# One core, attention and a mixture of experts: a longer ring of loaded tiles, one more border between batches, and last steps taken in another order

## What is computed

```python
x = layernorm(x + attention(x, W_Q, W_K, W_V))
logits = (x @ gate_w + gate_b) / 0.9
keep = the two experts with the highest logits
h = gelu(einsum('bsd,edf->bsef', x, w1) + b1)
y = einsum('bsef,efd->bsed', h, w2) + b2
f = sum over the kept experts of gate_prob * y
f = (f - mean) / sqrt(var + 1e-5) * ln_g + ln_b
out = layernorm(x + f)
```

## Time and profile before

| what | us |
|---|---|
| median of three runs (lowest, highest) | 259.19 (258.05, 260.06) |
| the profiled execution, its time | 257.17 |
| its span, first to last instruction | 255.4 |
| PE busy | 229.6 (90%) |
| DVE busy | 173.4 (68%) |
| ACT busy | 179.3 (70%) |
| POOL busy | 144.3 (57%) |

### The profile page before, as it was taken

How to read it: one execution, slowest core, us unless ns; L and a number is a source line. 1 busy time by engine, 2 the same in 40 slices (tenths; PEclk the granted TensorE clock), 3 DMA queues, 4 the chain that set the end, 5 groups by cost and what they waited for, 6 DMA issues and landing times.

```text
span 255.4 us, 7300 instructions
## 1 busy us (share of the span) xinstructions
PE 229.6 (90%) x1874; PEld 209.0 (82%) x1875; DVE 173.4 (68%) x958; ACT 179.3 (70%) x527; POOL 144.3 (57%) x165
## 2 busy tenths in 40 slices
PE   6988998999999799999999999999999999999100
PEld 3466876788787689999999999999999999999100
DVE  0146576787888888558953333366488999989884
ACT  3365857778675889977886555555555996599953
POOL 8400007357777777777877777775544545546500
PEclk9999999999999999999999999999999999999855
DMA  5999303023131545523328797868789686913275
GB/s 143 250 332 332 105 3 93 31 74 97 53 95 53 137 134 120 144 68 107 95 75 254 204 355 241 221 183 246 228 267 356 186 232 180 320 47 114 92 220 151
DMA packets 45105, 42.38 MB, mean 166 GB/s; under 512 B 5488, under 2 KB 34080, under 8 KB 45072
## 3 DMA queue, kind: packets, MB, share of 16 engines
q1 hardware_dynamic: 40224, 32.84, 45.2%
q0 software_dynamic: 4320, 8.92, 10.0%
q10 hardware_dynamic: 528, 0.26, 0.3%
HBM read 27.89 MB, written 12.01 MB: 156 GB/s over the span
## 4 chain that ended last, share of the span: by engine, by line
PE 78%; DVE 10%; ACT 5%; DVEq 2%; issue 2%; DMA 1%; ACTq 0%; SPq 0%
PE bank L595 26%; PE bank L584 25%; PE bank L435 6%; PE bank L462 4%; PE bank L502 3%; PE bank L421 3%; PE bank L483 2%; ACT rows L668 2%; PE bank L450 2%; ACT probs L676 2%; PE bank L426 2%; PE bank L592 2%; PE bank L416 1%; DMA wk<-in_L_attn_W_K_dram 1%; DVE sum_stats L1139 1%
## 5 line engine op out<-in xcount | busy, mean ns | idle before, releaser
L749 ACT ACTIVATE h<-bank,b_cols 128x128 f32<-128x128 f32 x284 | 81.6, 385 | 37.4 <-PE bank L584 37.0
L1340 POOL DMA_INDIRECT returned<-x,slot_back x71 | 71.3, 1004 | 43.0 <-DVE x L1120 33.2
L1335 POOL DMA_INDIRECT slots<-rows,slot_of x64 | 65.0, 1016 | 53.0 <-DVE rows L984 34.4
L595 PE MATMUL bank<-w_all,h 128*128 x568 | 78.5, 282 | 0.0
L584 PE MATMUL bank<-slot_xT,w_now 128*128 128x128 f32 x568 | 75.2, 275 | 0.1
L595 PEld LDWEIGHTS bank<-w_all,h 128*128 128x128 f32 x568 | 69.0, 192 | 0.8
L584 PEld LDWEIGHTS bank<-slot_xT,w_now 128*128 128x128 f32 x568 | 69.1, 192 | 0.3 <-DVE slot_xT L883 0.3
L881 DVE CAST slot_back<-slot_x 128x1 uint32<-128x1 f32 x71 | 10.4, 147 | 37.9 <-PE bank L584 37.8
L838 DVE TENSOR_REDUCE negmax<-bank 128x1 f32<-128x128 f32 (+3 forms) x32 | 14.7, 484 | 16.0 <-PE bank L436 15.8
L462 PEld LDWEIGHTS bank<-v,probsT 128*128 128x128 f32 x160 | 19.7, 192 | 5.7 <-issue 3.8
L1120 DVE TENSOR_SCALAR x<-bank,slot_gate 128x128 f32<-128x128 f32 x71 | 24.0, 341 | 0.2 <-PE bank L595 0.2
(11 more groups left out here) (155 smaller groups left out, 305.4 us busy)
## 6 DMA issues: line engine op xcount, KB each, us to landing
w_now<-in_L_ffn_w_dram SPq DMA_DIRECT2D x47, 256.0 KB, 3.6
slot_x<-slots SPq DMA_DIRECT2D x71, 65.0 KB
w_all<-in_L_ffn_w_dram SPq DMA_DIRECT2D x16, 256.0 KB, 5.9
pair<-returned SPq DMA_DIRECT2D x14, 256.0 KB, 3.2
rows<-rows SPq DMA_DIRECT2D x8, 256.0 KB, 3.0
x<-n_L_attn_embeddings_dram SPq DMA_DIRECT2D x7, 256.0 KB, 3.9
returned<-x,slot_back POOLq DMA_INDIRECT x71, 3.4
slots<-rows,slot_of POOLq DMA_INDIRECT x64, 2.3
```

The source lines that it names most:

```text
L595: m = nc.tensor.matmul(o, h[:, s % RING, c * P:(c + 1) * P], w2_c, start=False, stop=(c == FC - 1))
L749: m = nc.scalar.activation(h[:, s % RING, cols], bank_[:, cols], ACT.Gelu, bias=b1_cols[:, c:][:, bass.ds(first, 1)])
L1335: g_.indirect_dma_start(slots, bass.IndirectOffsetOnAxis(ap=slot_of[:, b, c:c + 1], axis=0), rows[:, k, b * TB + t, :], None).then_inc(dis ...
L1340: g_.indirect_dma_start(returned, bass.IndirectOffsetOnAxis(ap=slot_back[:, j:j + 1], axis=0), y[:, j % Y_RING, :], None).then_inc(y_retur ...
```

## The change

- The ring of loaded tiles has 24 places, not 8. The two small copies of `copy_slots` go: `weigh` and `give_back` read the gate and the row number from the loaded tile itself. For that the row numbers are written as integers. SP waits for the tile copy where it waited for the two small ones, and from tile 24 on also for the return of the tile 24 before.
- PE's loop over tiles 24 to 63 becomes straight-line code.
- A border after batch 4 is added (`WHOLE`: 39, 47, 55, 63, 67, 71), and the pairs of batches 4 and 5 are loaded ahead of tiles 62 and 70 (before: 70 and, for batch 5, behind the last tile's load).
- DVE's units begin a step later, take seven units of cost a step, stand in another order, and now hold batch 6's head; it goes out of `last_steps`.
- ACT's second root comes at tile 64, not 65.
- PE contracts tile 67 ahead of the expansion of tile 70, not behind it.

```diff
-    PARTS = (4 * 2, 6 * 2, 7 * 2, 7 * 2 + 1, 8 * 2)
+    PARTS = (4 * 2, 5 * 2, 6 * 2, 7 * 2, 7 * 2 + 1, 8 * 2)
...
-        slot_x = sb("slot_x", [P, UNROLL, ROW])
-        slot_back = sb("slot_back", [P, J], U32)
-        slot_gate = sb("slot_gate", [P, 2 * UNROLL])
+        SLOT_RING = 3 * UNROLL
+        slot_x = sb("slot_x", [P, SLOT_RING, ROW])
...
-        LOAD_AT = {b: WHOLE[0] + 15 + b for b in range(4)} | {b: WHOLE[1] + 10 + b for b in (4, 5)}
+        LOAD_AT = {b: WHOLE[0] + 15 + b for b in range(4)} | {b: WHOLE[b - 3] + 14 for b in (4, 5)}
...
-        FINAL_AT, FINAL_SHARE = WHOLE[0] + 7, 6
-        NORM_FROM, NORM_AT, OUT_AT, ROOT_AT = 2 * TB, 55, 67, (52, 65)
+        FINAL_AT, FINAL_SHARE = WHOLE[0] + 8, 7
+        NORM_FROM, NORM_AT, OUT_AT, ROOT_AT = 2 * TB, 55, 67, (52, 64)
...
-                    sp.wait_ge(slot_read, j - (UNROLL - 1))
+                    sp.wait_ge(slotT_ready, j - (UNROLL - 1))
                     sp.sem_inc(wait_held, 1)
+                    if j >= SLOT_RING:
+                        sp.wait_ge(y_returned[(j - SLOT_RING) % Y_RING], 16 * ((j - SLOT_RING) // Y_RING + 1))
...
-                    load_slots(s, at[s])
+                    load_slots(j % SLOT_RING, at[s])
...
-                            if b in (0, FIRST):
-                                wait_whole(0 if b < FIRST else 1)
+                            if b == 0 or b >= FIRST:
+                                wait_whole(max(b - 3, 0))
...
+                    if last and s == LAST - 1:
+                        contract(J - LAG, (J - LAG) % UNROLL, e[s + 1]).then_inc(step_done, 1)
...
-            with pe.Fori(BOUND, BODIES - 1) as i:
+            for i in range(BOUND, BODIES - 1):
                 body(i, late=True)
             body(BODIES - 1, late=True, last=True)
             e = expert_numbers(J, LAG)
-            for s in range(LAG):
+            for s in range(1, LAG):
                 contract(J - LAG + s, (J - LAG + s) % UNROLL, e[s]).then_inc(step_done, 1)
...
-                vec.tensor_copy(slot_back[:, bass.ds(j, 1)], slot_x[:, s % UNROLL, BACK:ROW])
-                vec.tensor_copy(slot_gate[:, j % (2 * UNROLL):j % (2 * UNROLL) + 1], slot_x[:, s % UNROLL, GATE:BACK]).then_inc(slot_read, 1)
                 vec.tensor_copy(slot_xT[:, s % RING, :], psT_of(j, s)).then_inc(slotT_ready, 1)
...
-                vec.tensor_scalar(y[:, j % Y_RING, :], psY(s), slot_gate[:, j % (2 * UNROLL):j % (2 * UNROLL) + 1], None, ALU.mult).then_inc(y_ready, 1)
+                vec.tensor_scalar(y[:, j % Y_RING, :], psY(s), slot_x[:, j % SLOT_RING, GATE:BACK], None, ALU.mult).then_inc(y_ready, 1)
...
-            FINAL += [(what, b, cost) for b in (2, 3) for what, cost in PLAIN]
-            FINAL += [(what, b, cost) for b in (4, 5) for what, cost in HEAD]
-            FINAL += [("centre", 4, 5), ("centre", 5, 5), ("root", 1, 3)]
+            FINAL += [(what, 2, cost) for what, cost in PLAIN]
+            FINAL += [(what, 4, cost) for what, cost in HEAD]
+            FINAL += [(what, 3, cost) for what, cost in PLAIN]
+            FINAL += [("centre", 4, 5)] + [(what, 5, cost) for what, cost in HEAD] + [("centre", 5, 5), ("root", 1, 3)]
             FINAL += [(what, b, cost) for b in (4, 5) for what, cost in FUSED[1:]]
+            FINAL += [(what, 6, cost) for what, cost in HEAD]
...
             def last_steps():
                 for q in range(finished_by(J), len(FINAL)):
                     final_unit(q)
-                add_pair(6)
-                take_moments(6)
                 finish_root(2)
...
-                g_.indirect_dma_start(returned, bass.IndirectOffsetOnAxis(ap=slot_back[:, j:j + 1], axis=0),
+                g_.indirect_dma_start(returned, bass.IndirectOffsetOnAxis(ap=slot_x[:, j % SLOT_RING, BACK:ROW].bitcast(U32), axis=0),
```

More of the change, by code:

```diff
@@ L219, in moe_block @@
         slot_loaded = [sem(f"slot_loaded{s}") for s in range(UNROLL)]
-        slot_read = sem("slot_read")
         wait_held = sem("wait_held")
@@ L304, in load_slots @@
             def load_slots(s, at):
-                sp.dma_start(slot_x[:, s, :], slots[bass.ds(at, P), :]).then_inc(slot_loaded[s], 16)
+                sp.dma_start(slot_x[:, s, :], slots[bass.ds(at, P), :]).then_inc(slot_loaded[s % UNROLL], 16)
             def load_pair(b):
@@ L392, in _ @@
                 load_w1(J - W1_LAG + k, e)
-            wait_whole(2)
+            wait_whole(3)
             load_pair(B - 2)
-            wait_whole(3)
+            wait_whole(4)
             load_pair(B - 1)
-            wait_whole(4)
+            wait_whole(5)
             load_pair(B)
@@ L501, in transpose_slots @@
                     pe.wait_ge(y_ready, i * UNROLL + (s - AHEAD - LAG - 3))
-                return nc.tensor.transpose(psT_of(i if not isinstance(i, int) else i * UNROLL + s, s), slot_x[:, s, 0:D], ident[:])
+                return nc.tensor.transpose(psT_of(i * UNROLL + s, s), slot_x[:, (i * UNROLL + s) % SLOT_RING, 0:D], ident[:])
             def step(b):
@@ L607, in body @@
                 tiles = LAST if last else UNROLL
-                e = expert_numbers(i * UNROLL, tiles)
+                e = expert_numbers(i * UNROLL, tiles + (1 if last else 0))
                 for s in range(FIRST_EXPANDED if first else 0, tiles):
@@ L744, in gelu @@
             def gelu(j, s, first):
-                act.wait_ge(step_done, j + 1)
+                act.wait_ge(step_done, j + 1 + (1 if isinstance(j, int) and j == J - 1 else 0))
                 bank_ = psH_first[s] if isinstance(j, int) and j < UNROLL else psH[s % 4]
@@ L1114, in weigh @@
             def weigh(i, s):
-                dve.wait_ge(step_done, i * UNROLL + (s + LAG + 1))
                 j = i * UNROLL + s
+                dve.wait_ge(step_done, j + LAG + (0 if j == J - LAG else 1))
                 if j >= Y_RING:
                     dve.wait_ge(y_returned[j % Y_RING], 16 * (j // Y_RING))
-                vec.tensor_scalar(y[:, j % Y_RING, :], psY(s), slot_gate[:, j % (2 * UNROLL):j % (2 * UNROLL) + 1], None, ALU.mult).then_inc(y_ready, 1)
+                vec.tensor_scalar(y[:, j % Y_RING, :], psY(s), slot_x[:, j % SLOT_RING, GATE:BACK], None, ALU.mult).then_inc(y_ready, 1)
             one = "p (t a) -> p t a"
@@ L1206, in final_unit @@
                     m = aggregate(b)
-                    if (b, again) in ((3, False), (5, False), (5, True)):
+                    if (b, again) in ((3, False), (5, False), (5, True), (6, False)):
                         m.then_inc(aggregated, 1)
@@ L1313, in _ @@
             for b in range(B):
-                g_.iota(rows[:, :, b * TB:(b + 1) * TB, BACK], [[N, TOPK], [1, TB]], base=b * S, channel_multiplier=TB,
+                g_.iota(rows[:].bitcast(I32)[:, :, b * TB:(b + 1) * TB, BACK], [[N, TOPK], [1, TB]], base=b * S, channel_multiplier=TB,
                         allow_small_or_imprecise_dtypes=True).then_inc(const_ready, 1)
@@ L1320, in _ @@
             pool.wait_ge(made, 4)
-            g_.iota(empty[:, :, BACK], [[P, BLOCKS]], base=TOPK * N, channel_multiplier=1,
+            g_.iota(empty[:].bitcast(I32)[:, :, BACK], [[P, BLOCKS]], base=TOPK * N, channel_multiplier=1,
                     allow_small_or_imprecise_dtypes=True).then_inc(const_ready, 1)
```

## The result

The changed kernel takes 260.36 us in the median of 20 runs (259.27 to 262.31), the kernel before beside it 258.68 us (257.04 to 260.39). The ratio is 1.0078, interval 1.0055 to 1.0101: it became 1.4 to 2.6 us slower, within the 1% named in the prediction, but clearly not a gain.

A forecast was written before the change was run, and what follows sets the result against it. TensorE's 2.005 us a tile bounds it to the last contraction, then VectorE's tail. Adding 0.2 for ScalarE's root, 0.1 for the table and 0.1 for pair 8 to the 259.19 us median gives 259.6, range 257.6 to 261.8.

The forecast's parts named there:

- rival C: TensorE at tiles 24 and 25: both loads 0.4 us late, both stall, + 0.5; time 260.0 to 260.7 us; chance 0.11.
- Ring, straight line, pace: Tile loop: ring saves VectorE 0.13 us a step, TensorE nothing; straight line costs nothing, pace stays 2.005 us a tile.
- Rival E: TensorE's tile loop: its four jumps back cost fetches, so straight-line code gives back 8.8 us; time 250.8; chance 0.03.
- Rival D: VectorE's steps: removing the copies saves nothing, tile 62's weighing slips 2.6 us, end 2.7 later, 261.9 us; chance 0.12.
- The head buys a wait: VectorE's tail: batch 6's head, moved earlier, only gains a 1.1 us wait for ScalarE's square root for batch 6.
- 1 us later than now: TensorE's contractions of tiles 69 and 70 wait for weighings of tiles 65 and 66, ending 1 us later, about 238.1.
- a wait of about 1 us: Sign of being right: VectorE waits about 1 us ahead of root 3's reciprocal, until ScalarE's square root ends it.
- B: VectorE's tail: with ScalarE's root early, 1.99 us shorter, but pair 8 then ends the wait; 258.4 us; chance 0.14.
- The tail's size: Tail after the last tiles: 0.3 us longer, 0.2 for ScalarE's root and 0.1 for pair 8.
- the prediction's term of 0.1: Batch 8's add in VectorE's tail: its pair lands at 248.0 against 247.9, adding 0.1 us.
- The table: Tile table ready 0.7 us later by the added border, delaying tile 24's load; 0.1 us taken, range 0 to 0.5.
- the two bounds: Tile 24's load: on time if it takes 1.8 us or less, 0.4 late if it takes 2.2.

The follow-up runs named there:

- E23: Not a run: the start of TensorE's expansion of tile 23, a point from which stretches of the profiles are compared.
- E66: Not a run: the start of TensorE's expansion of tile 66; 224.34 us in the kernel before, 227.86 in the changed kernel.
- x4: Changed kernel with batch 6's add, stats and aggregate put back behind the last weighing; ratio 1.0039 to the kernel before.
- x5: Changed kernel with ScalarE taking root 3 ahead of the eight early normalisations, roots 4 and 5 ahead of batch 5's late ones; ratio 1.008 to the kernel before.
- x11: Changed kernel with GpSimd's first three returns behind the last batch's dispatch, not ahead of it; ratio 1.008 to the kernel before.
- x12: Changed kernel with batch 6's head among the last weighings, ScalarE's root 3 earlier, last dispatch before returns, tile 24's load before the table wait; ratio 1.0002 to the kernel before.
- x13: Changed kernel with the copy of batch 6's rows issued behind the loads of tiles 6 and 7; ratio 1.0073 to the kernel before.
- E3: Not a run: the start of TensorE's expansion of tile 3; 96.42 us in the kernel before, 99.14 in the changed kernel.
- E1: Not a run: the start of TensorE's expansion of tile 1; 92.71 us in the kernel before, 94.98 in the changed kernel.
- x6: Kernel before with loop written out, ring of 24, batch 6's head among the last three weighings, ScalarE's root 3 before early normalisations; ratio 0.9967.
- x14: The x6 kernel with the copy of batch 6's rows also moved behind the loads of tiles 6 and 7; ratio 0.9994 to the kernel before.
- x3: Kernel before with only TensorE's loop over tiles 24 to 63 written out; 259.46 us, ratio 1.005.
- x2: Kernel before with the loop written out and the ring of 24, five borders and the old units; ratio 0.9987.

## Why the prediction was right, and where its sum was not

The forecast (259.6 us, + 0.4 on what was before) named the verdict and the tail's mechanism; the loss is about 2.0. Of that, 0.84 came in the tail, 0.80 by rival C, which had a chance of 0.11, and 0.45 at a place that the prediction doesn't have. TensorE did wait ahead of tiles 24 and 25, the sign named for C, and 260.36 lies in C's 260.0 to 260.7. That the forecast's time is only 0.8 off is in part luck: it starts from 259.19, where the runs beside the changed kernel gave 258.68. Step by step:

**Ring, straight line, pace: right.** 86.21 us for the 43 tiles from E23 to E66 is 2.005 each. Rival E is out: with the loop's jumps gone the pace is the same. Rival D is out too: tile 62 was weighed at 228.2 (3.52 us taken off), where 228.0 was foretold and D had 2.6 more. The Trainium skill, "Runtime: NRT & Kernel Launch", section "Instruction fetch mechanics", has a taken branch outside the fetch window stall; no run here shows it for this loop. Nor does the even pace speak against that rule, as the prediction had it. The queue q8 carries more blocks of instructions once TensorE's loop is written out: none from 153 to 226 us in the kernel before, 7 in the straight line alone. If it is TensorE's queue, as that suggests, the loop fetched nothing from its second pass on, and its jumps went to code that was there.

**The head buys a wait: right, nearly to the step.** With the 3.52 us taken off:

| step | foretold | measured |
|---|---|---|
| tile 62 weighed | 228.0 | 228.2 |
| pair 6 issued | 231.0 | 231.2 |
| batch 6's add, its wait | 234.4, 1.1 | 234.8, 1.56 |
| last contraction ends | 238.1 | 239.0 |
| scatter 70 | 242.8 | 242.8 |
| reciprocal of root 3, its wait | 241.0, 1.1 | 241.05, 0.23 |
| batch 8's add | 248.0 | 248.2 |

Two misses in it cancel. The last contraction was set at "1 us later than now"; but it follows the weighing of tile 66 at 236.8, and 0.34 for that weighing with 1.4 for bias and products gives 238.5 by the prediction's own terms; it was 239.0. VectorE was thus busy nearly a us longer and waited that much less for ScalarE: 0.23 us, where the prediction named a wait of about 1 us as its sign. The reciprocal stood where ScalarE put it, as foretold (root 3 done at E66 + 16.67 us instead of 16.45, gelu of tile 70 started 0.3 later), and the x4 run confirms it: the head's place doesn't move it (16.71 and 16.70). B's condition was met in x5, and pair 8 took over the wait, as B had it.

**The tail's size: 0.3 foretold, 0.84 measured.** 0.46 is there at batch 8's add (root 0.2, pair 8 0.16, the rest small), against 0.3 foretold. The other 0.38 comes behind it, and it repeats: from that add to the end it is 7.9 to 8.1 us in the five profiles in which the add waits for pair 8 (the changed kernel, x5, x11, x12, x13) and 7.5 to 7.9 in the seven in which it doesn't. Each of the five has a gap of 0.22 us between the last two aggregations, to which the profile gives no cause, and none of the seven has it there. So a pair 8 that comes late goes with more than its own wait, which the prediction's term of 0.1 didn't hold; why stays open.

**The table: the step that was mis-sized.** 0.1 was taken from a range of 0 to 0.5; it is 0.80. The mechanism is that of rival C. Since TensorE is 0.45 late from tile 3 on, the lateness of the loads is read from E3 (96.42 before, 99.14 after). Tile 24's load goes out at E3 + 34.75 us instead of 34.06: 0.69 later, where 0.7 was foretold, and in the chain such a load takes 1.9, inside the 1.8 to 2.2 of the two bounds. Its wait of 0.13 is thus the prediction's 0.1. Three things were missing. First, a stall costs TensorE 0.19 more than the wait, twice. Second, tile 25's load is 1.05 later (E3 + 37.28 instead of 36.23) where 0.5 was foretold: the last dispatch starts 0.59 later, about as foretold, but from its start to the load's issue it is 3.07 us instead of 2.61. Third, this load was put under the same bounds as tile 24's, as if one stall covered both; but the two tiles are late by different things, as x11 shows, and tile 25 waits 0.30 on top of what tile 24 has cost. So 0.13 + 0.19 + 0.30 + 0.19 makes the 0.80 (0.81 in rounded terms).

The lengthening of GpSimd's scatters was foretold from the earlier trace rows and came: 2.77 and 3.09 us, while VectorE's two products of 1 x 2208 ran from 122.55 and 125.94, 2.45 us each. The first of them, and the sum behind both (VectorE's timeline):

```profile
122.55 2.45 DVE L1051 TENSOR_TENSOR passed<-tile_start,ends 1x2208 f32<-1x2208 f32 x1
...
128.93 2.44 DVE L1058 TENSOR_REDUCE steps<-passed 1x46 f32<-1x2208 f32 x1
```

The Trainium skill, "SBUF — State Buffer", section "Who interferes with whom", says that a VectorE instruction with both inputs in SBUF and a GpSimd instruction that reads SBUF exclude each other. These rows agree for the two products. The sum, as long as they but with one input, held nothing up: the scatters that began beside it at 129.53 and 130.80 took 0.96 and 0.97 us.

**Tile 3: not in the sum at all, 0.45 us.** In both kernels tile 6's load is issued 0.27 us behind E1, just behind the copy of batch 6's rows (256 KB). Its packets end at about E1 + 2.1 us before and E1 + 3.0 after. A view of the DMA queues from E1 + 0.2 to E1 + 1.9, changed kernel, has one thing more (packets, MB, share of 16 engines):

```profile
q1 hardware_dynamic: 543, 0.27, 59.7%
q0 software_dynamic: 31, 0.07, 14.5%
q8 instruction: 1, 0.02, 5.2%
```

The same stretch of the kernel before:

```profile
q1 hardware_dynamic: 587, 0.29, 62.5%
q0 software_dynamic: 25, 0.04, 6.9%
```

It is a block of 16 KB of a program. With the straight line q8 carries 17 such blocks instead of 11. In the changed kernel, x4, x5, x11, x12 and x13 this block falls 0.3 to 1.3 us behind E1, in the others 3.3 to 4.0; E1 to E3 is 4.03 to 4.63 us in the five of the former with the copy in its old place, and 3.40 to 3.71 in the latter, the kernel before among them. In x13 the block lies at E1 + 0.5 and the stretch is 3.59, as the load was long done. The copy ahead of the load, before and then changed (KB, us from issue to landing):

```profile
rows<-rows SPq DMA_DIRECT2D x1, 256.0 KB, 2.8
...
rows<-rows SPq DMA_DIRECT2D x1, 256.0 KB, 4.2
```

Its packets show how: 480 of 512 have ended by E1 + 1.9 us in both, and the last 32, a sixteenth, end by 1.9 before and at 2.4 to 3.2 in the changed kernel. It is so in all six profiles with the early block, x13 among them (2.0 to 3.5), and in none of the other six. That is what a block on one of the 16 DMA engines would do to that engine's share; the profile doesn't give a packet's engine. Why the block comes earlier stays open.

## What to carry to other kernels

An operation that is moved ahead gains only if everything that its successor waits for comes earlier too: list each engine's releaser at the next meeting point (here ScalarE's root, then the returns) before counting the operation's length. A lateness on two queues that feed consecutive tiles is two stalls and adds up, and a stall costs TensorE more than its wait (here 0.19 us more each). When profiles of one kernel scatter at the start, compare them from a later event.

## What the runs showed of the hardware

**The start.** The eight products of L426 take 2.05 us in the one profile and 1.13 in the other. The first record of TensorE's granted clock in a trace stands between 8.0 and 13.6 us: 8.03 before, 8.34 with the head back (x4), 13.47 after, 13.51 in x6, 13.43 in x14. It shows the upper level (2.4 GHz). A stretch ahead of it has no record and reads 1.00 in the profile's slices, but the products there are slow. TensorE's timeline has the same product (128x512, bf16) before, then after:

```profile
8.31 0.38 PE L549 MATMUL bank<-idle 128*128 128x512 bf16 x1
...
8.94 0.63 PE L549 MATMUL bank<-idle 128*128 128x512 bf16 x1
```

At 6.08 us, ahead of the record, it took 0.63 in the kernel before as well, so there, too, the upper level is shown from 8.03 us on only. In x5, recorded from 8.86, it takes 0.38 at 8.88, and in x3, recorded from 9.41, 0.63 at 8.87. So the start scatters with the time at which the clock goes up, after a first 8 us in which TensorE was busy for 6.0 us before and 5.6 after. Tile 1 starts later with it: at 92.7 to 92.9 us where the record stands at 8.0 to 8.1 (before, x12), at 95.0 to 95.3 where it stands at 13.4 to 13.6 (after, x6, x11, x14). No pattern by kernel is to be seen in that. The spans of three kernels with the same time from E1 to the end (before, x3, x2) go with their starts: 255.4, 256.1 and 256.5 us for 92.71, 93.60 and 94.15. A start 2.3 us later is most of the 3.4 us by which the run times of the kernel before differ (257.04 to 260.39), which would fit, but only one of these runs has its start recorded.

**A dip.** In x5 tile 1 is late (94.92 us) though its clock is recorded from 8.86. The stretch of 40 to 50 us shows another cause (us, PE, PEld, DVE, ACT, POOL busy with counts, granted clock, DMA share, GB/s):

```profile
30.00:40.00 10.00, 9.97 (x75) 8.02 (x74) 7.00 (x49) 5.23 (x14) 1.38 (x2) 1.00 0.10 29
40.00:50.00 10.00, 8.71 (x54) 7.06 (x53) 7.01 (x44) 6.69 (x19) 6.57 (x7) 0.83 0.26 80
```

The 0.83 is a mean: the clock is granted at its lower level (1.2 GHz, 0.50) from 46.4 to 49.8 us, and products of L462 take 421 ns there and 280 elsewhere in this profile. TensorE was busy for 8.74 of the 10 us ahead of it. The kernel before shows 1.00 in the same stretch. x3 and x4 have such a dip of 3.4 us too, at 87.9 and 86.9 us, the other nine profiles none. So the granted clock of each stretch is looked at before two profiles are compared.

**Instruction blocks and data.** The straight line loads 0.28 MB of instructions on q8 instead of 0.18, and the place of one block goes with 0.9 us at a load of 65 KB and with a landing of the copy 1.4 us later, as above. The Trainium skill, "Runtime: NRT & Kernel Launch", section "Instruction fetch mechanics", gives 16 KiB blocks that a queue of the engine's own fetches, mostly hidden; the size agrees with the trace.
